# Turning x in a ring of four banks ahead of the edge counting, one-hots with the tile innermost, and window bounds loaded one window ahead

## The chip, the cores and the metric

The kernel runs on one core of a Trainium2 chip. The metric is the time of one execution on the device in microseconds. The text calls the engines by the names of the profile: PE is TensorE's matrix array and PEld its weight load, DVE is VectorE, ACT is ScalarE, POOL is GpSimd and SP is SyncE. Each engine has a sequencer that works through its instructions in order and hands the arithmetic to the engine behind it; register operations, branches and loads into registers are done by the sequencer itself.

## The reference

The graph has 1024 nodes and 16384 edges, sorted by destination. Two graph networks follow each other, each with a residual and a layer norm.

```python
edge_index = jnp.stack([src, dst])                     # 16384 edges, dst sorted
x = _layernorm(x + gat_two_layers(x, W1, a_src1, a_dst1, b1, W2, a_src2, a_dst2, b2, edge_index))
x = _layernorm(x + gcn_two_layers(x, W1, b1, W2, b2, edge_index))   # self loops, x 1024 x 768

def gat_layer(x, W, a_s, a_d, b, edge_index, concat):
    h = (x @ W).reshape(n, H, C)                       # first layer: 8 heads of 768
    alpha_s, alpha_d = einsum(h, a_s), einsum(h, a_d)
    e = leaky_relu(alpha_s[src] + alpha_d[dst], 0.2)
    e = exp(e - segment_max(e, dst)[dst])
    alpha = e / (segment_sum(e, dst)[dst] + 1e-16)
    return segment_sum(h[src] * alpha, dst) + b

def gcn_conv(x, W, b, src, dst, n_nodes):
    h = x @ W
    norm = dinv[src] * dinv[dst]                       # dinv = 1 / sqrt(degree)
    return segment_sum(h[src] * norm, dst) + b
```

The kernel never gathers by edge. It first builds a dense table countT of how many edges go from each source to each destination, and every later sum over edges is a matmul with that table.

## The kernel before

The change lies in the first stage, `graph_and_heads`, which does two things before its large matmuls: it counts the edges, and it turns x.

**Counting.** The edges lie in 128 tiles of 128, one edge per partition. From each edge two keys are made. The low key is the source modulo 128. The other key holds the block of the source and the destination; it is compared against 512 lanes for each of 16 windows of 64 destinations (`WD`, `NW`). A one-hot of the low key is the stationary operand and a one-hot of the other key the moving one of a 128x128 by 128x512 matmul, and the sum over the edge tiles that can touch the window is the window's part of countT. All low one-hots are made before the first window: `hot_low` is a table of 128 columns for each tile, in groups of 8 tiles (`TG`). ACT makes the first `ACT_TILES` tiles, a group in two steps: 8 times |lane - key| into `far` (L473), then one Relu of 1 - far over 128x1024 (L478). DVE makes the rest with one comparison over 128x1024 for each group (L737). The other one-hots, `hot_key`, are made by DVE window by window, in two buffers, 8 firm tiles (L749) and then pairs of tiles in a loop (L754) whose end is read from a register; in most windows this loop runs once.

**PE's part of a window** (from L1066): two loads of registers from `range_i`, the first tile and the end of the loop (L1067, L1068, each `value_load` is a load, a register operation and an assertion); 8 matmuls (L1076); a loop of pairs of matmuls (L1080, L1083); and a small matmul with zeros that closes the sum (L1085). ACT then copies the window's bank to countT (L511). DVE's part has the same two loads in front (L744, L745).

**Turning x.** x is needed with its features on the partitions, in two parts, xTh (rounded) and xTl (what is left). There are 12 groups g of 128x512 (6 blocks of features, 2 halves of the nodes). For each, PE turns four blocks of x into bank g modulo 4 (`turn_x`, L1047), ACT copies the bank to xTh (`x_high`, L487), PE subtracts xTh from the bank (`lessen_x`, L1055), and ACT copies what is left to xTl (`x_low`, L491). `turn_x(g)` for g of 4 and more waits until `x_low(g - 4)` has emptied the bank. Three groups are turned before the first window (`X_BEFORE`); then window w turns group w + 3 and lessens group w, after its closing matmul.

**Order.** Each engine runs its instructions in the order written. PE, before the counting, waits for ACT's last column copy (L506, behind all of ACT's low one-hots), turns three groups, then waits for both engines' low one-hots. The tables of lanes are written by POOL's iota instructions at the very start (L440 to L442), followed by the identity (L443, L445), which PE needs for every transpose and so for the keys. After the last window PE waits for countT and starts the large matmuls of q = 0 (L1106), in which 12 column blocks by 8 row blocks follow each other. The remaining stages (attention, second layer, graph convolution) are bound to that start by their data.

## Time and profile before

| | us |
|---|---|
| median of three timed runs | 1778.51 |
| lowest and highest of them | 1774.86, 1779.06 |
| the profiled execution, whole time | 1777.28 |
| its span, first to last instruction | 1775.2 |
| PE busy in the span | 1673.4 (94%) |
| first matmul of x's turning | 19.37 |
| closing matmul of the first window | 25.97 |
| closing matmul of the last window | 79.11 |
| first large matmul (L1106) | 80.09 |

The span is counted from the first instruction, and all times of the trace are offsets from it. The chain of waits in the page is almost wholly PE's, so a microsecond in front of 80.09 is a microsecond of the whole. A stretch of the trace is best read in the order of time, engine by engine; the sequencer's own instructions stand under PEldq and DVEq in the view of one source line.

### The profile page before, as it was taken

The page shows a single profiled execution, that of the slowest core. Times are in us where ns is not written, and L with a number is a line of the kernel's source. Part 1 is how long each engine was busy: PE and PEld are TensorE (multiplying, and loading weights), DVE is VectorE, ACT ScalarE, POOL GpSimd, SP SyncE. Part 2 cuts the span into 40 slices and gives each one's busy share as a digit, 9 for nine tenths or more (in the row PEclk, how much of TensorE's full clock was granted, in tenths as well). Part 3 has the DMA queues.
Part 4 walks back from the last instruction along what each step waited for, and adds up shares of the span by engine and source line. Part 5 has one row for each costly group of instructions (what it writes and reads, how often), then busy time and mean ns, then how long its engine had stood idle before and what let it go on. Part 6 is the DMA issues. An engine that isn't in the chain of part 4 may idle for free. (4 is left out here: it accounts for less than half of the span.)

```text
span 1775.2 us, 21747 instructions
## 1 busy us (share of the span) xinstructions
PE 1673.4 (94%) x7596; PEld 1393.4 (78%) x7601; DVE 1223.8 (69%) x2336; ACT 798.1 (45%) x1295; POOL 164.7 (9%) x117
## 2 busy tenths in 40 slices
PE   5899999999979999999999899999999975879998
PEld 3588888788857888888888688888888864878898
DVE  8744454654787887788877687888767348974447
ACT  6333321222545565565555455655556225534240
POOL 0023221312200000000000000000000013210003
PEclk9999999999989999999999999999999977989999
DMA  3155575766535765557654765666344321131222
GB/s 135 42 184 184 180 235 167 172 226 205 199 114 197 191 185 148 149 176 213 173 125 173 198 158 160 178 187 168 122 171 182 112 110 36 54 127 55 63 83 105
DMA packets 133808, 268.04 MB, mean 151 GB/s; under 512 B 23738, under 2 KB 83524, under 8 KB 121028
## 3 DMA queue, kind: packets, MB, share of 16 engines
q1 hardware_dynamic: 133700, 266.63, 48.8%
q8 instruction: 63, 1.03, 0.2%
q14 instruction: 45, 0.37, 0.1%
HBM read 206.21 MB, written 60.40 MB: 150 GB/s over the span
## 5 line engine op out<-in xcount | busy, mean ns | idle before, releaser
L41 PE MATMUL bank<-ph,hc 128*128 128x512 f32 x768 | 300.2, 391 | 4.7 <-DMA hc<-h_scratch 3.5
L43 PE MATMUL bank<-ph,hc 128*128 128x512 f32 x768 | 299.5, 390 | 0.0
L42 PE MATMUL bank<-pl,hc 128*128 128x512 f32 x768 | 299.4, 390 | 0.0
L771 DVE CUSTOM_DVE_ANT_0 junk<-bank,a_bc 128x512 bf16<-128x512 f32 (+1 forms) x256 | 129.9, 554 | 195.3 <-ACT st L523 180.1
L41 PE MATMUL bank<-hh,w2h 128*128 128x512 f32 x576 | 226.2, 393 | 14.7 <-DVE w2l L853 10.3
L41 PE MATMUL bank<-wh,xTh 128*128 128x512 f32 x570 | 224.3, 393 | 4.7 <-POOL wl L458 4.7
L43 PE MATMUL bank<-hh,w2l 128*128 128x512 f32 x576 | 225.7, 392 | 0.0
L42 PE MATMUL bank<-hl,w2h 128*128 128x512 f32 x576 | 225.5, 392 | 0.0
L43 PE MATMUL bank<-wh,xTl 128*128 128x512 f32 x570 | 223.3, 392 | 0.0
L42 PE MATMUL bank<-wl,xTh 128*128 128x512 f32 x570 | 223.1, 391 | 0.0
L41 PEld LDWEIGHTS bank<-ph,hc 128*128 128x128 f32 x768 | 144.5, 188 | 36.0 <-DMA hc<-h_scratch 3.9
L43 PEld LDWEIGHTS bank<-ph,hc 128*128 128x128 f32 x768 | 144.5, 188 | 30.1
L42 PEld LDWEIGHTS bank<-pl,hc 128*128 128x128 f32 x768 | 144.6, 188 | 30.0
L591 ACT ACTIVATE he<-mean,bias 128x512 f32<-128x512 f32 x96 | 69.6, 725 | 213.4 <-DVE mean L914 213.4
L523 ACT CAST st<-bank 128x512 fp32r<-128x512 f32 x96 | 56.5, 589 | 226.3 <-PE bank L43 218.2
L41 PEld LDWEIGHTS bank<-hh,w2h 128*128 128x128 f32 x576 | 109.2, 190 | 38.4 <-issue 10.7
L41 PEld LDWEIGHTS bank<-wh,xTh 128*128 128x128 f32 x570 | 107.9, 189 | 28.0 <-POOL wl L458 5.6
L42 PEld LDWEIGHTS bank<-hl,w2h 128*128 128x128 f32 x576 | 109.1, 189 | 22.9
L43 PEld LDWEIGHTS bank<-hh,w2l 128*128 128x128 f32 x576 | 109.0, 189 | 23.0
L43 PEld LDWEIGHTS bank<-wh,xTl 128*128 128x128 f32 x570 | 107.7, 189 | 22.6
L42 PEld LDWEIGHTS bank<-wl,xTh 128*128 128x128 f32 x570 | 107.8, 189 | 22.2
L914 DVE TENSOR_TENSOR mean<-bank,rden 128x512 f32<-128x512 f32 x96 | 66.0, 687 | 83.4 <-PE bank L43 83.4
(257 smaller groups left out, 2867.6 us busy)
## 6 DMA issues: line engine op xcount, KB each, us to landing
hc<-h_scratch SPq DMA_DIRECT2D x96, 1024.0 KB, 5.4
h_scratch<-st SPq DMA_DIRECT2D x96, 512.0 KB, 3.0
w2r<-in_L_gnn_W SPq DMA_DIRECT2D x96, 384.0 KB, 6.6
wr<-in_L_gnn_W SPq DMA_DIRECT2D x12, 1536.0 KB, 8.7
gwr<-in_L_gnn_W SPq DMA_DIRECT2D x24, 384.0 KB, 3.2
row_bc<-logits_scratch SPq DMA_DIRECT2D x16, 512.0 KB, 13.1
expo_bc<-expo_scratch SPq DMA_DIRECT2D x16, 512.0 KB, 6.2
xr<-in_x SPq DMA_DIRECT2D x2, 1536.0 KB, 8.4
```

What stands on the lines that cost most here:

```text
L41: nc.tensor.matmul(out, sh, mh, start=first, stop=False, skip_group_check=not grouped)
L42: nc.tensor.matmul(out, sh, ml, start=False, stop=False, skip_group_check=not grouped)
L43: return nc.tensor.matmul(out, sl, mh, start=False, stop=last, skip_group_check=not grouped)
L523: nc.scalar.copy(st[n % 4][:, :, 0, :], banks[n % 6][:, :].rearrange("p (g c) -> p g c", g=4)).then_inc(main_hi, 1)
L591: nc.scalar.activation(he[:, g % 2, :], mean[:, g % 2, :], ACT.Exp, bias=b)
L771: nc.vector.tensor_tensor_reduce(out=junk[:, s % 2, 0:hi - lo], in0=banks[n % 6][:, lo:hi], in1=a_bc[q % 2][:, k, lo:hi], scale=1.0, scala ...
L914: nc.vector.tensor_tensor(mean[:, g % 2, :], banks[6 + g % 2][:, :], rden[:, :], ALU.mult).then_inc(a_out, 1)
```

## The change

The diff does six things.

- **ACT makes 24 tiles of low one-hots rather than 32**, and DVE 104 rather than 96.
- **hot_low has the tile innermost.** The element of tile t and column l lies at l * 128 + t rather than t * 128 + l. ACT's Relu reads `far` with a step of 128 elements and writes runs of 8; DVE's comparison writes runs of 8, and reads a written-out table `lanes` (128 lanes, each 8 times, 16 bits) and `key16`, the low key in 16 bits, 8 elements again and again. PE's weight load takes 128 columns with a step of 128 elements.
- **The lane table** costs an iota of 128x1024 on POOL, in front of the identity's last step, and a cast to 16 bits on DVE, in front of upto_end. `key16` costs ACT one more copy of the key's bank.
- **x is turned in a ring of four.** Before the first window PE turns groups 0 to 3, lessens 0 to 3 and turns 4 to 7, behind the keys but no longer behind ACT's column copies. Then window w lessens group w + 4 (w below 8) and, after that, turns group w + 8 (w below 4).
- **The bounds of a window** are loaded one window ahead on PE and DVE, between the 8 firm tiles and the loop.
- ACT's order follows: x_high 0 to 3, x_low 0 to 3, x_high 4 to 7, and in window w, behind the copy to countT, x_low(w + 4) and x_high(w + 8).

```diff
-ACT_TILES = 32
+ACT_TILES = 24
-    hot_low = put("hot_low", 86016, [P, 2 * ET, P], BF16)
+    hot_low = put("hot_low", 86016, [P, 2 * ET * P], BF16)
+    lane_t = put("lane_t", early + 13312, [P, P, TG], I32)
+    lanes = put("lanes", early + 17408, [P, P, TG], F16)
+    key16 = put("key16", early + 19456, [P, P], F16)
-    X_BEFORE = 3
+    XA = 4
+    def low_tiles(j):
+        return hot_low[:, 0:P * ET].rearrange("p (l t) -> p l t", t=ET)[:, :, j * TG:(j + 1) * TG]
...
             nc.gpsimd.memset(ident[:, :], 0.0).then_inc(const_g, 1)
+            nc.gpsimd.iota(lane_t[:, :, :], pattern=[[1, P], [0, TG]], base=0, channel_multiplier=0).then_inc(lanes_made, 1)
             pool.wait_ge(const_g, 4)
...
             def low_hot_end(j):
                 act.wait_ge(far_done, j + 1)
-                nc.scalar.activation(hot_low[:, j * TG:(j + 1) * TG, :].rearrange("p t l -> p (t l)"), far[:, j % 2, :, :].rearrange("p t l -> p (t l)"),
+                nc.scalar.activation(low_tiles(j), far[:, j % 2, :, :].rearrange("p t l -> p l t"),
                                      ACT.Relu, bias=ones[:, 0:1], scale=-1.0).then_inc(low_hot_s, 1)
...
             nc.scalar.copy(keyT[:, 1, 0:P], banks[5][:, 0:P]).then_inc(key_out, 1)
+            nc.scalar.copy(key16[:, :], banks[5][:, 0:P]).then_inc(key16_out, 1)
...
-            for g in range(X_BEFORE):
+            for g in range(XA):
+                x_high(g)
+            act.wait_ge(range_done, 9)
+            for g in range(XA):
+                x_low(g)
+            for g in range(XA, 2 * XA):
                 x_high(g)
             for w in range(NW):
                 act.wait_ge(count_full, w + 1)
                 nc.scalar.copy(countT[:, :, w * WD:(w + 1) * WD], count_bank(w)[:, :].rearrange("p (s d) -> p s d", s=NB)).then_inc(count_out, 1)
-                if w < XG:
-                    if w + X_BEFORE < XG:
-                        x_high(w + X_BEFORE)
-                    x_low(w)
+                if w + XA < XG:
+                    x_low(w + XA)
+                if w + 2 * XA < XG:
+                    x_high(w + 2 * XA)
...
+            dve.wait_ge(lanes_made, 1)
+            nc.vector.tensor_copy(lanes[:, :, :], lane_t[:, :, :]).then_inc(lanes_made, 1)
             dve.wait_ge(const_v, 3)
             nc.vector.tensor_scalar(upto_end[:, :], upto[:, :], -1.0, float(EP), ALU.mult, ALU.add).then_inc(const_v, 1)
...
             for j in range(ACT_TILES // TG, ET // TG):
-                nc.vector.tensor_tensor(hot_low[:, j * TG:(j + 1) * TG, :],
-                                        lane[:, 0:P].unsqueeze(1).to_broadcast([P, TG, P]),
-                                        keyT[:, 1, j * TG:(j + 1) * TG].unsqueeze(2).to_broadcast([P, TG, P]), ALU.is_equal).then_inc(low_hot_v, 1)
+                nc.vector.tensor_tensor(low_tiles(j), lanes[:, :, :], key16[:, j * TG:(j + 1) * TG].unsqueeze(1).to_broadcast([P, P, TG]),
+                                        ALU.is_equal).then_inc(low_hot_v, 1)
...
-            pe.wait_ge(range_done, 9)
-            pe.wait_ge(cols_done, 3)
             pe.wait_ge(low_out, 1)
             pe.wait_ge(const_c, 4)
-            for g in range(X_BEFORE):
+            for g in range(XA):
                 turn_x(g)
+            for g in range(XA):
+                lessen_x(g)
+            for g in range(XA, 2 * XA):
+                turn_x(g)
+            pe.wait_ge(range_done, 9)
+            following = bounds(0)
+            pe.wait_ge(cols_done, 3)
             pe.wait_ge(low_hot_s, ACT_TILES // TG)
             pe.wait_ge(low_hot_v, (ET - ACT_TILES) // TG)
             for w in range(NW):
-                first = pe.value_load(range_i[w:w + 1, 0:1], min_val=0, max_val=ET - SLOTS)
-                pairs = pe.value_load(range_i[w:w + 1, 1:2], min_val=FIRM // 2 + 1, max_val=EP)
+                first, pairs = following
...
-                    mm = nc.tensor.matmul(bank[:, :], hot_low[:, bass.ds(first + j, 1), :].rearrange("p t l -> p (t l)"), hot_key[w % 2][:, j, :],
+                    mm = nc.tensor.matmul(bank[:, :], hot_low[:, bass.ds(first + j, P, ET)], hot_key[w % 2][:, j, :],
                                           start=(j == 0), stop=False, skip_group_check=True)
...
+                if w + 1 < NW:
+                    following = bounds(w + 1)
                 with pe.Fori(FIRM // 2, pairs) as q:
...
-                if w < XG:
-                    if w + X_BEFORE < XG:
-                        turn_x(w + X_BEFORE)
-                    lessen_x(w)
+                if w + XA < XG:
+                    lessen_x(w + XA)
+                if w + 2 * XA < XG:
+                    turn_x(w + 2 * XA)
```

DVE's window loop is changed as PE's is: its two loads go behind the eight firm tiles.

## Rows read from the trace of the kernel before

**Rows 1.** PE in order of time, windows that turn x: start, length, instruction, tiles.
```profile
36.20 0.22 PE L1085 MATMUL bank<-zero_b 128*128 128x128 bf16 x1
...
37.12 0.48 PE L1055 MATMUL bank<-xTh,neg_ident 128*128 128x512 f32 x1
...
39.77 0.22 PE L1085 MATMUL bank<-zero_b 128*128 128x128 bf16 x1
```
**Rows 2.** PE in order of time, the last window and the close before it, without x.
```profile
75.76 0.22 PE L1085 MATMUL bank<-zero_b 128*128 128x128 bf16 x1
76.94 1.90 PE L1076 MATMUL bank<-hot_key,hot_low 128*128 128x512 bf16 x8 [0.96 <-ACT countT L511]
...
79.11 0.22 PE L1085 MATMUL bank<-zero_b 128*128 128x128 bf16 x1
```
**Rows 3.** PE's source lines, one window: durations min/median/max in ns, first and last start.
```profile
L1067 PEldq TENSOR_LOAD <-range_i x1: 306/306/306, 72.1 to 72.1; - x1
...
L1076 PEldq FUSED_REGOPS  x8: 55/55/60, 73.5 to 74.4; - x8
L1076 PEld LDWEIGHTS bank<-hot_key,hot_low x8: 95/97/97, 73.6 to 74.9; 128*128 x8
...
L1080 PEldq COMPARE_BRANCH  x1: 70/70/70, 75.2 to 75.2; - x1
```
**Rows 4.** PE in order of time, the long window's closing matmul and one two windows later.
```profile
44.29 0.22 PE L1085 MATMUL bank<-zero_b 128*128 128x128 bf16 x1
...
52.00 0.22 PE L1085 MATMUL bank<-zero_b 128*128 128x128 bf16 x1
```
**Rows 5.** ACT in order of time, behind the closing matmul at 36.20.
```profile
36.45 0.59 ACT L511 CAST countT<-bank 128x512 int16<-128x512 f32 x1 [0.87 <-PE bank L1085]
37.40 0.59 ACT L487 CAST xTh<-bank 128x512 fp32r<-128x512 f32 x1 [0.36 <-PE bank L1047]
37.88 0.59 ACT L491 CAST xTl<-bank 128x512 fp32r<-128x512 f32 x1
```
**Rows 6.** POOL and then DVE in order of time, the tables and the first key.
```profile
0.83 0.55 POOL L440 IOTA lane_i<- 128x512 int32 x1 [0.39 <-POOLq L1887]
1.35 0.44 POOL L441 IOTA pair_i<- 16x128 int32 x1
...
1.95 0.43 DVE L685 CAST lane<-lane_i 128x512 f16<-128x512 int32 x1
...
3.39 0.23 DVE L695 TENSOR_SCALAR parts_i<-edge_i 128x128 int32<-128x128 int32 x1
```
**Rows 7.** ACT in order of time, its low one-hots and its last column copy.
```profile
5.17 4.78 ACT L473 ACTIVATE far<-lane,keyT 128x128 f16<-128x128 f16 x16
...
16.90 2.17 ACT L478 ACTIVATE hot_low<-far,ones 128x1024 bf16<-128x1024 f16 x2
...
19.11 0.16 ACT L506 COPY gcn_bias<-bank 128x6 f32<-128x6 f32 x1
```
**Rows 8.** PE in order of time, x's first three groups and the first window's close.
```profile
19.37 4.54 PE L1047 MATMUL bank<-ident,xr 128*128 128x128 f32 x24 [12.56 <-ACT gcn_bias L506]
...
25.97 0.22 PE L1085 MATMUL bank<-zero_b 128*128 128x128 bf16 x1
```
**Rows 9.** DVE in order of time, its low one-hots and eight firm tiles of a window.
```profile
8.02 13.69 DVE L737 TENSOR_TENSOR hot_low<-lane,keyT 128x1024 bf16<-128x1024 f16 x12
...
34.99 2.19 DVE L749 TENSOR_SCALAR hot_key<-lane,keyT 128x512 bf16<-128x512 f16 x8 [0.31 <-issue]
```
**Rows 10.** The tile xr, its two loads: last line is DMA from issue to landing, min/median/max.
```profile
L352 SPq DMA_DIRECT2D xr<-in_x x2: 401/454/507, 3.2 to 3.6; - x2
...
DMA to landing us min/median/max: 6.7/8.4/10.2
```
**Rows 11.** Windows of PE at a pause: stretch and length, busy (instructions), granted clock, DMA.
```profile
316.00:318.76 2.76, 0.61 (x4) 1.00 0.88 294
318.76:323.20 4.44, 4.44 (x12) 0.62 0.00 0
```

More of the change, by code:

```diff
@@ L236, in graph_and_heads @@
     hot_free = [sem(f"hot_free{w}") for w in range(NW)]
-    x_less = sem("x_less")
+    x_less, lanes_made, key16_out = sem("x_less"), sem("lanes_made"), sem("key16_out")
     count_full, count_out = sem("count_full"), sem("count_out")
@@ L733, in _, with bounds @@
             nc.vector.tensor_copy(range_i[:, :], range_f[:, 2:4]).then_inc(range_done, 1)
[L735 removed]
+            dve.wait_ge(key16_out, 1)
+            dve.wait_ge(lanes_made, 2)
             for j in range(ACT_TILES // TG, ET // TG):
[L737 to L739 removed]
+                nc.vector.tensor_tensor(low_tiles(j), lanes[:, :, :], key16[:, j * TG:(j + 1) * TG].unsqueeze(1).to_broadcast([P, P, TG]),
+                                        ALU.is_equal).then_inc(low_hot_v, 1)
             dve.wait_ge(range_done, 9)
             dve.wait_ge(low_out, 1)
+            def bounds(w):
+                return (dve.value_load(range_i[w:w + 1, 0:1], min_val=0, max_val=ET - SLOTS),
+                        dve.value_load(range_i[w:w + 1, 1:2], min_val=FIRM // 2 + 1, max_val=EP))
+            following = bounds(0)
             for w in range(NW):
[L744 to L745 removed]
+                first, pairs = following
                 if w >= 2:
@@ L1056, in lessen_x, with bounds @@
                                  start=False, stop=True, skip_group_check=True).then_inc(x_less, 1)
-            pe.wait_ge(range_done, 9)
-            pe.wait_ge(cols_done, 3)
+            def bounds(w):
+                return (pe.value_load(range_i[w:w + 1, 0:1], min_val=0, max_val=ET - SLOTS),
+                        pe.value_load(range_i[w:w + 1, 1:2], min_val=FIRM // 2 + 1, max_val=EP))
             pe.wait_ge(low_out, 1)
             pe.wait_ge(const_c, 4)
-            for g in range(X_BEFORE):
+            for g in range(XA):
                 turn_x(g)
+            for g in range(XA):
[3 more added lines that the diff above has]
+            pe.wait_ge(range_done, 9)
+            following = bounds(0)
+            pe.wait_ge(cols_done, 3)
             pe.wait_ge(low_hot_s, ACT_TILES // TG)
@@ L1066, in _ @@
             for w in range(NW):
-                first = pe.value_load(range_i[w:w + 1, 0:1], min_val=0, max_val=ET - SLOTS)
-                pairs = pe.value_load(range_i[w:w + 1, 1:2], min_val=FIRM // 2 + 1, max_val=EP)
+                first, pairs = following
                 bank = count_bank(w)
@@ L1079, in _ @@
                         mm.then_inc(hot_free[w + 1], SLOTS)
+                if w + 1 < NW:
+                    following = bounds(w + 1)
                 with pe.Fori(FIRM // 2, pairs) as q:
@@ L1082, in _ @@
                         pe.wait_ge(hot_ready[w], q * 2 + (j + 1))
-                        nc.tensor.matmul(bank[:, :], hot_low[:, bass.ds(q * 2 + first + j, 1), :].rearrange("p t l -> p (t l)"), hot_key[w % 2][:, FIRM + j, :],
+                        nc.tensor.matmul(bank[:, :], hot_low[:, bass.ds(q * 2 + first + j, P, ET)], hot_key[w % 2][:, FIRM + j, :],
                                          start=False, stop=False, skip_group_check=True).then_inc(hot_free[w], 1)
                 nc.tensor.matmul(bank[:, 0:P], zero_b[:, 0:P], zero_b[:, 0:P], start=False, stop=True, skip_group_check=True).then_inc(count_full, 1)
-                if w < XG:
-                    if w + X_BEFORE < XG:
-                        turn_x(w + X_BEFORE)
-                    lessen_x(w)
+                if w + XA < XG:
+                    lessen_x(w + XA)
+                if w + 2 * XA < XG:
+                    turn_x(w + 2 * XA)
             pe.wait_ge(x_lo, XG)
```

3 lines of the change are left out of this document (removed).

## The prediction

> **What bounds the kernel now.** I read the page first: its chain of waits is PE from end to end. The part that the change touches ends with the last window's closing matmul at 79.11 [rows 2]; one copy later PE starts its large matmuls, and what follows is fed from there, so I count a shift of that row one for one. The timeline from 0 to 85 us shows two stretches: a preparation that ends with the first window's closing matmul at 25.97 [rows 8], and the counting.
>
> Within the counting, the first windows, which turn x, close 3.45 us apart (four from 25.97 to 39.77) [rows 1, 8], and windows without x 3.35 apart (75.76 to 79.11) [rows 2]. Nearly the same, though the first kind has over 1 us more of matmul work. The view of PE's source lines explains it. In one window without x the first register load starts at 72.1, the eight firm matmuls get their addresses from 73.5 to 74.4, and the loop's branch comes at 75.2 [rows 3]. The sequencer is at work throughout: some 1.3 us for the two bounds, 1.1 for the eight firm tiles, 0.8 for the loop and the close, with rounding 3.35. It waits for nobody. Outside the x windows the bound is thus PE's sequencer, not its array, and the reader should see that the array's idle time in front of L1076 is the price of instructions, not of a wait.
>
> DVE makes its eight firm tiles in 2.19 us [rows 9] and with pair and loads stays below PE's period; it is not the bound.
>
> **Part 1: bounds loaded one window ahead.** This moves two loads in a sequencer that never waits in such a window. Its work stays 3.35, so the period stays 3.35. Three things are gained. The last window carries no loads any more: between its predecessor's close and its own lie ten matmuls and a start (from 76.94 to 79.11 are 2.17) [rows 2], 2.4 us, so -0.95. The one window with a second pass of the loop is followed today by two disturbed ones: from 39.77 to 52.00 [rows 1, 4] are 12.23 us, where three regular windows take 10.35. The second pass itself, 44.29 less 39.77 less 3.45 [rows 1, 4], is 1.1 us and stays; the other 0.8 is the loads of PE and DVE standing in line behind it, and goes. Windows 8 to 11, which carry parts of x today and will not, save up to 0.1 each, 0.3 together. The gain is 0.95 + 0.8 + 0.3, some 2.0 us. As bounds: none of it (0), or, were the loads hidden altogether in the seven windows up to the last but one, 0.3 more in each, since DVE's own period (2.19, and some 0.8 around it) is then next: 4.1.
>
> **Part 2: the ring of four banks.** Here I expect the loss. Today window w turns group w + 3, whose bank was emptied one window earlier. After the change window w lessens group w + 4 and then turns group w + 8 into the same bank. The turn must wait until ACT has emptied it, and ACT starts that copy, x_low(w + 4), only behind the copy of this very window to countT, which waits for the closing matmul. The new wait stands on PE, and all of the next window is queued behind it, address work and matmuls. Its length from the closing matmul: 0.25 until ACT starts (36.20 to 36.45) [rows 1, 5], 0.48 from one ACT copy to the next (37.40 to 37.88) and 0.59 for x_low [rows 5], and 0.10 from the end of an ACT copy to PE's next start (19.11 and 0.16 to 19.37) [rows 7, 8]: 1.42. Only then can the sequencer go on with the window's 3.24 us of loads, tiles, loop and close. The period is 4.7. The array alone would need 1.42, 0.87 for the turn (36.20 to 37.12 are 0.92, with some 0.05 of the closing matmul) [rows 1] and 2.17 for ten matmuls [rows 2], 4.5, so the sequencer still decides. Four periods at 4.7 stand where 13.8 us stood: +5.0. If the array's figure decides, +4.2; if the wait were hidden wholly, 0. I take 5.0, since each term is a row.
>
> **Part 3: the tables.** The new iota stands in front of the identity on POOL, and its cast on DVE in front of the keys. An iota of 512 elements in one run takes 0.55 us, 1.1 ns an element; pair_i, 128 elements in runs of two, takes 0.44, 3.4 ns an element [rows 6]. The new one has 1024 elements in 128 runs of 8. Bounds: 1.1 and 3.5 us. With 1.0 ns an element and some 4.5 a run, which fits both rows, it is 1.6; I take that, as its runs lie between the two. It starts near 1.9 and ends at 3.5. The cast then holds DVE for 0.60 (twice the elements of L685, whose 0.43 has about 0.15 of start) [rows 6], three small instructions take 0.5, and L695 starts at 4.7 rather than 3.39 [rows 6]: the keys are 1.3 late (0.8 to 3.2). Both chains of one-hots hang on them. The copy to key16 is short and lies in ACT's wait for its own first copy; I count 0, at most 0.2.
>
> **Part 4: ACT's chain to the first window.** ACT drops a group of 8 far (0.30 each, 4.78 for 16) and a Relu (1.04, half of the 2.17 for two) [rows 7]: -3.4. With the keys 1.3 late its last column copy ends near 17.1, not 19.27. Today PE waits for that copy and turns x from 19.37 [rows 8]. After the change PE turns groups 0 to 3 when x's first half lands, at 3.2 + 6.7 = 9.9 [rows 10], under ACT's one-hots. But x_high(0) still stands behind these, at 17.2. Four x_high at 0.48 bring x_low(0) to 19.1 and its end to 19.7, and turn 4 starts at 19.85. Four turns at 0.87 are 3.5 us. The first window could start at 23.4, and its close, held by the sequencer's first loads behind x_low(3), come at 25.85: -0.1 against 25.97 [rows 8]. The 2 us that ACT gained are used up by the ring's first round.
>
> The clock adds to that. PE's first turns ran at the lower rate: 24 in 4.54 us [rows 8], where eight later ones, one group, take 0.87 [rows 1]. After a stretch in which PE was busy for 0.61 of 2.76 us, the mean granted clock of the next 4.44 us was 0.62 [rows 11], mostly the 1.2 of the two levels, 1.2 and 2.4 GHz. The new kernel has turned its four groups by about 15.2 and pauses until the first lessening at 17.9, 2.7 us. I expect the same fall; over the turns of groups 4 to 7 it costs about 1.2 us. The first window starts at 24.6 and its ten matmuls close at 26.8: +0.85. That is my value; -0.1 is the other end.
>
> **Part 5: the new layout.** DVE's comparisons are 12 in 13.69 us, 1.14 apart, and 16-bit work at another line makes 512 elements in 0.27 (2.19 for eight) [rows 9], so 1024 cost at least 0.5. Thirteen take 6.9 to 14.8 us from 9.3 on and end between 16 and 24.1. I take 0.6 each and an end at 17, as all operands become runs of 16-bit elements like those of that row. Either way ACT's chain, 24.6, is later: DVE's gain is off the path, and the slow end costs up to 0.7. For ACT's Relu with a step of 128 elements there is no row: between no change and twice its time per element I take no change. PE's weight load takes 97 ns [rows 3] under a matmul of 217 (2.17 us for ten) [rows 2]; with its new step I take it as hidden.
>
> On this layout the Trainium skill, "Advanced Engine Details and Errata", section SBUF Cachelines, speaks against the change: full rate needs another access in the same 16-byte line, and a new line for each access is slower. By it the Relu's reads and PE's weight columns, one element a line, would pay; no run here shows such a step yet. On DVE's comparison the skill's "Vector Engine (DVE) Microarchitecture Reference", section 5.1, says that two-source work on 2-byte elements at step 1 yields two a cycle; at its 0.96 GHz that is, as an estimate, 0.53 us and a start.
>
> **The sum.** Preparation +0.85, ring +5.0, windows -2.0: +3.9 us. Against the profiled execution's 1777.28 this is 1781.2. The median of the runs, 1778.51, lies 1.2 above that execution, and the forecast for a median is 1782.4.
>
> **The rivals.** *The forecast*, a net 1 to 5.3 us, 0.59.
> *Strided reads cost ACT (slower).* A Relu's time per element is 1.04 less 0.30 over the 896 elements that it has beyond a far [rows 7], 0.83 ns. If each costs twice, three Relus are 0.85 longer, +2.6 us, all on the chain to x_high(0): 1785.0. It decides the verdict from 0.5 us a Relu on. For it: each read is 256 bytes from the last; against it: no row shows a cost. 0.22.
> *The weight load becomes the bound (slower).* Up to 217 ns it hides, and up to 0.33 the sequencer's 3.35 covers it. At 0.45 each window's ten need 4.5: +1.2 in twelve windows, 1796. 0.05.
> *The ring's wait is hidden (no change).* Part 2 is then 0: 1777.4, and 1776.5 without the fall of the clock. For it: PE's sequencer runs ahead of its array. Against it: the wait starts at the closing matmul itself. 0.09.
> *The loads are hidden too (faster).* With Part 1 at -4.1, the ring hidden and the preparation at -0.1 it is 1774.3. 0.05.
>
> 0.3%, about what a measurement of this kernel can tell from no change, is 5.3 us. The forecast lies inside, with about a sixth beyond the edge; the slower rivals go mostly beyond: slower 0.32, faster 0.05, within 0.63. The range for 8 in 10 takes in the iota's upper bound or the Relus above and a hidden ring below: 1776.5 to 1788.
>
> **What would show it.** Closing matmuls 4.7 apart in the first four windows, with turns (L1047) that wait for ACT's copy to xTl; 3.35 apart in the last eight although the loads stand elsewhere; 2.4 before the last; L695 near 4.7; comparisons 0.6 apart; the first closing matmul at 26.8, and a granted clock below 1.00 between 19 and 22. The prediction is wrong if the first periods are near 3.5, if the last fall towards 3.0 (then the sequencer was not the bound), or if Relus or weight loads grow.

## The result, and the profile after

The changed kernel takes 1787.51 us (median; 1784.28 to 1789.29) where the kernel before takes 1778.51. The ratio is 1.0049, interval 1.0037 to 1.0061: 9 us slower. The forecast was 3.9 us slower. The direction is the forecast's, and 1787.5 is inside the range of 1776.5 to 1788, though by half a microsecond only. The loss is 2.3 times the forecast's, and beyond the 0.3% within which the prediction had put its 0.63.

The profiled execution of the changed kernel has a span of 1785.9 us, and the first large matmul starts at 88.41 instead of 80.09. These 8.3 us account for nearly all of the 9.0 between the medians. These are the marks of the two traces beside those of the prediction (us from the span's start; the predicted fifth and last are added up from its first closing matmul, its period of 4.7 and its gain of 2.0):

| mark | before | predicted | after |
|---|---|---|---|
| first key instruction | 3.39 | 4.7 | 5.08 |
| first closing matmul | 25.97 | 26.8 | 30.99 |
| fifth closing matmul | 39.77 | 45.6 | 49.78 |
| last closing matmul | 79.11 | 82.9 | 87.42 |

From first to fifth the change costs 4.99 us (forecast 5.0), from fifth to last it gains 1.70 (forecast 2.0). The preparation costs 5.02 where the forecast had 0.85. That is where the prediction missed.

**The tables.** POOL and DVE in order of time; [rows 6] answer to it. Columns in all timelines: start, length, engine, line, instruction.
```profile
1.31 2.16 DVE L694 CAST ones_r<-ones 128x128 fp32r<-128x128 f32 x1
...
1.92 1.82 DVE L698 CAST lane<-lane_i 128x512 f16<-128x512 int32 x1
1.99 1.40 POOL L450 IOTA lane_t<- 128x1024 int32 x1
...
3.96 0.68 DVE L702 CAST lanes<-lane_t 128x1024 f16<-128x1024 int32 x1
...
5.08 0.21 DVE L710 TENSOR_SCALAR parts_i<-edge_i 128x128 int32<-128x128 int32 x1
```
The iota takes 1.40 us (estimate 1.6). Two DVE casts that were begun when it started both end just behind its end: the cast of lane takes 1.82 us instead of 0.43 [rows 6].

**ACT, DVE and PE up to the first window.** In order of time; [rows 7 to 9] answer to it.
```profile
6.84 4.78 ACT L480 ACTIVATE far<-lane,keyT 128x128 f16<-128x128 f16 x16
...
9.68 7.92 DVE L753 TENSOR_TENSOR hot_low<-lanes,key 128x1024 bf16<-128x1024 f16 x13
10.02 5.30 PE L1068 MATMUL bank<-ident,xr 128*128 128x128 f32 x32 [1.54 <-DMA xr<-in_x]
...
11.53 2.09 ACT L485 ACTIVATE hot_low<-far,ones 128x1024 bf16<-128x1024 f16 x1
...
16.00 3.98 ACT L485 ACTIVATE hot_low<-far,ones 128x1024 bf16<-128x1024 f16 x2
...
20.71 2.25 PE L1076 MATMUL bank<-xTh,neg_ident 128*128 128x512 f32 x4 [5.39 <-ACT xTh L494]
...
22.75 5.70 PE L1068 MATMUL bank<-ident,xr 128*128 128x128 f32 x32
...
30.99 0.22 PE L1116 MATMUL bank<-zero_b 128*128 128x128 bf16 x1
```
A far costs what it did, 0.30 us. A Relu, the instruction at L485, takes about 2.05 us where [rows 7] have two in 2.17. DVE's thirteen comparisons take 7.92 us, 0.6 each, and end at 17.6; PE's first window, which needs them, starts at 28.29. PE pauses for 5.39 us in front of its first lessening, and its turns of groups 4 to 7 then take 5.70.

The granted clock tells why. Stretches of PE: length, busy (instructions), granted clock, DMA.
```profile
15.00:19.70 4.70, 0.32 (x3) 1.00 1.04 350
19.70:22.70 3.00, 1.99 (x4) 0.54 0.20 74
22.70:26.50 3.80, 3.80 (x19) 0.50 0.00 0
```
0.50 is the 1.2 GHz level. Stretches cut at finer times show it from 19.97, 0.7 us before PE's restart, to 26.80, and 1.00 behind that.

**The ring.** PE and then ACT around the second closing matmul; [rows 1, 5] answer to it.
```profile
35.73 0.22 PE L1116 MATMUL bank<-zero_b 128*128 128x128 bf16 x1
35.76 0.48 PE L1076 MATMUL bank<-xTh,neg_ident 128*128 128x512 f32 x1
37.11 1.16 PE L1068 MATMUL bank<-ident,xr 128*128 128x128 f32 x8 [0.87 <-ACT xTl L498]
```
```profile
35.98 0.59 ACT L524 CAST countT<-bank 128x512 int16<-128x512 f32 x1 [1.44 <-PE bank L1116]
36.47 0.59 ACT L498 CAST xTl<-bank 128x512 fp32r<-128x512 f32 x1
```
The turn starts 1.38 us behind the closing matmul (working: 1.42) and waits for ACT's copy to xTl. The first four periods are 4.74, 4.66, 4.64 and 4.75.

**The windows without x.** PE's firm matmuls in one such window by source line (ns min/median/max), then the last window in order of time; [rows 3] and [rows 2] answer.
```profile
L1105 PEld LDWEIGHTS bank<-hot_key,hot_low x12: 208/208/211, 75.9 to 79.8; 128*128 x12
L1105 PEldq FUSED_REGOPS  x10: 46/46/53, 76.0 to 79.4; - x10
```
```profile
85.00 0.22 PE L1116 MATMUL bank<-zero_b 128*128 128x128 bf16 x1
85.14 2.02 PE L1105 MATMUL bank<-hot_key,hot_low 128*128 128x512 bf16 x7
...
87.42 0.22 PE L1116 MATMUL bank<-zero_b 128*128 128x128 bf16 x1
```
The weight load has doubled, from 97 to 208 ns, and stays just below the matmul's 217. The address instruction has become cheaper, 46 ns for 55. The period is 3.26 to 3.28 instead of 3.35, the last one 2.42.

### The profile page after: what moved, and what is told of

It reads as the page before. It is cut to its first block and busy times, and to the rows that moved or that the text cites. A ratio compares the mean times of both kernels' runs of the same rounds, so it can differ in the third digit from the quotient of the medians.

```text
span 1785.9 us, 21744 instructions
## 1 busy us (share of the span) xinstructions
PE 1684.1 (94%) x7596; PEld 1413.5 (79%) x7601; DVE 1225.9 (69%) x2338; ACT 802.4 (45%) x1287; POOL 167.2 (9%) x118
## 5 line engine op out<-in xcount | busy, mean ns | idle before, releaser
L42 PEld LDWEIGHTS bank<-pl,hc 128*128 128x128 f32 x768 | 144.6, 188 | 29.9
```

Of the source, the lines that this page charges most:

```text
L42: nc.tensor.matmul(out, sh, ml, start=False, stop=False, skip_group_check=not grouped)
```

## The experiments

Each kernel was timed in three rounds against the kernel before on the same chip. The ratio is to the kernel before, with its 95% interval; the closing matmuls and the first large matmul are from the profiled execution.

| kernel | ratio | first | fifth | last close | large matmuls |
|---|---|---|---|---|---|
| before | 1 | 25.97 | 39.77 | 79.11 | 80.09 |
| changed | 1.0049 [1.0037, 1.0061] | 30.99 | 49.78 | 87.42 | 88.41 |
| ring_late | 1.0016 [1.0006, 1.0025] | 30.61 | 44.53 | 82.41 | 83.40 |
| relu_dense | 1.0058 [1.0042, 1.0075] | 34.60 | 53.30 | 90.88 | 91.87 |
| tables_late | 1.0036 [1.0023, 1.0048] | 30.27 | 48.86 | 86.51 | 87.49 |
| kept_warm | 1.0025 [1.0014, 1.0036] | 29.59 | 48.30 | 85.69 | 86.68 |
| loads_ahead | 0.9993 [0.9983, 1.0002] | 26.21 | 39.85 | 78.05 | 79.04 |
| loads_held | 1.0035 [1.0023, 1.0046] | 33.34 | 52.12 | 87.12 | 88.10 |
| recast | 0.9965 [0.9950, 0.9980] | 22.34 | 36.25 | 74.13 | 75.11 |
| recast_held | 0.9975 [0.9966, 0.9985] | 25.67 | 39.52 | 75.06 | 76.05 |
| layout_old | 1.0041 [1.0029, 1.0052] | 27.27 | 47.46 | 85.59 | 86.57 |
| recast_old | 0.9996 [0.9986, 1.0007] | 27.48 | 41.26 | 79.36 | 80.34 |
| recast_two | 0.9977 [0.9966, 0.9989] | 25.01 | 38.87 | 75.53 | 76.51 |

The last column less 80.09 and the difference in time that the ratio gives agree within about 2 us in every row (recast: -5.0 and -6.2; ring_late: +3.3 and +2.9; relu_dense: +11.8 and +10.3; kept_warm: +6.6 and +4.5). To within these 2 us a shift of the first large matmul is handed on to the time. The times alone do not part loads_ahead and recast_old from the kernel before, nor tables_late, loads_held, layout_old and relu_dense from the changed one; for these the closing matmuls speak. Spans of single profiled executions scatter more behind that point, and I rest nothing on them.

### The ring: the turn one window later

```diff
-                if w + XA < XG:
-                    lessen_x(w + XA)
-                if w + 2 * XA < XG:
-                    turn_x(w + 2 * XA)
+                if 1 <= w and w - 1 + 2 * XA < XG:
+                    turn_x(w - 1 + 2 * XA)
+                if w + XA < XG:
+                    lessen_x(w + XA)
```
(and ScalarE's x_high and x_low in the same order)

> The changed kernel with its turning moved one window later: window w turns group w + 7 (w from 1 to 4), whose bank was emptied in the window before, and then lessens group w + 4. Theory of the ring: PE no longer waits for ACT's copy to xTl behind its own closing matmul, so from the first to the fifth closing matmul it takes about 13.9 us rather than 18.8, the first large matmul comes 5 us earlier than in the changed kernel (near 83.4), and the time falls by about 5 us. Rival, the slower weight load (209 ns) fills the array in windows that turn x: the periods fall only to 3.7 or more, 14.8 in all. Rival, the periods are the address work's and the loads': nothing changes.

ring_late is 5.0 us less than the changed kernel at the first large matmul. The fence has PE and ACT in order of time around a window's start.
```profile
33.87 0.22 PE L1116 MATMUL bank<-zero_b 128*128 128x128 bf16 x1
33.93 1.11 PE L1068 MATMUL bank<-ident,xr 128*128 128x128 f32 x8
...
34.13 0.59 ACT L524 CAST countT<-bank 128x512 int16<-128x512 f32 x1 [1.45 <-PE bank L1116]
```
The turn now starts 0.06 us behind the close, into a bank that ACT emptied a window ago. Four periods are 13.92 us instead of 18.79. The ring's wait is the cause of these 4.9 us; the first closing matmul came 0.38 sooner besides.

### The Relu: reads in one run

```diff
-    far = put("far", early + 3072, [P, 2, TG, P], F16)
+    far = put("far", early + 3072, [P, 2, P, TG], F16)
...
-                    last = nc.scalar.activation(far[:, j % 2, i, :], lane[:, 0:P], ACT.Abs, bias=keyT[:, 1, tile:tile + 1], scale=-1.0)
+                    last = nc.scalar.activation(far[:, j % 2, :, i], lane[:, 0:P], ACT.Abs, bias=keyT[:, 1, tile:tile + 1], scale=-1.0)
...
-                nc.scalar.activation(low_tiles(j), far[:, j % 2, :, :].rearrange("p t l -> p l t"),
+                nc.scalar.activation(low_tiles(j), far[:, j % 2, :, :],
```

> The changed kernel with far laid out with the tile innermost, so that the Relu reads without a step and |lane - key| is written with a step of 8 elements (16 bytes); hot_low is written as before. Theory, the read at 256 bytes a step is what made the Relu 2.05 us: the three Relus are back at 1.13, far stays 0.30 each, ACT's chain is 2.8 us shorter and the first large matmul near 85.6. Rival, the runs of 8 that are written cost: Relus stay at 2.05, nothing moves. Rival, the cost goes over to the writes of far: Relus 1.13 but far 0.4 or more each, over 2.4 us back.

ACT in order of time:
```profile
6.84 9.45 ACT L480 ACTIVATE far<-lane,keyT 128x128 f16<-128x128 f16 x16
15.78 1.36 ACT L485 ACTIVATE hot_low<-far,ones 128x1024 bf16<-128x1024 f16 x1
...
21.52 2.37 ACT L485 ACTIVATE hot_low<-far,ones 128x1024 bf16<-128x1024 f16 x2
```
With reads in one run a Relu is 1.36, 1.34 and 1.13 us, so the 256-byte read step was its cost. The two longer ones start while the last far is still under way (the first at 15.78, where the fars end at 16.29). The third stands behind a Relu and takes the 1.13 of the kernel before, though it writes in runs of 8 like the others. But far, which now writes each element 16 bytes behind the last, goes from 0.294 to 0.54 us apiece. Twenty-four of these lose 5.9 us where the Relus gained 2.3, and the kernel is slower still: its first closing matmul comes at 34.60. This is the rival that had the cost go over to far. Of the two places tried the transposition costs less in the Relu, once for eight tiles.

### The table: POOL's iota behind the identity

```diff
+            nc.gpsimd.iota(lane_t[:, :, :], pattern=[[1, P], [0, TG]], base=0, channel_multiplier=0).then_inc(lanes_made, 1)
```
(moved from ahead of the identity's last step to behind it; its cast moved from ahead of the keys to ahead of the comparisons; ACT waits for it in front of x_low(0))

> The changed kernel with the lane table's iota behind the identity's last step on POOL and its cast to 16 bits on DVE just in front of the comparisons, behind the keys. Theory: the first key instruction is back near 3.4 (5.08 in the changed kernel), the cast of ones is back at 0.56 us (2.16), and the first window, which hangs on ACT's chain, starts 1.7 us earlier; the comparisons end where they did and stay off the path. The first large matmul is near 86.7. Rival: DVE's comparisons now decide and nothing is gained; rival: POOL's iota slows DVE's key instructions beside it, and part of the 1.7 stays.

POOL and DVE in order of time:
```profile
1.31 0.56 DVE L695 CAST ones_r<-ones 128x128 fp32r<-128x128 f32 x1
...
1.95 0.43 DVE L699 CAST lane<-lane_i 128x512 f16<-128x512 int32 x1
...
2.49 1.41 POOL L453 IOTA lane_t<- 128x1024 int32 x1
2.52 1.40 DVE L701 CAST win_f<-win_i 128x16 f32<-128x16 int32 x1
...
4.49 0.21 DVE L709 TENSOR_SCALAR parts_i<-edge_i 128x128 int32<-128x128 int32 x1
```
The casts of ones and lane are back at 0.56 and 0.43. Now the cast that happens to lie beside the iota stands: sixteen elements take 1.40 us, where the changed kernel needs 0.15 for them. So DVE does not merely queue behind the iota's result; a cast that has nothing to do with it waits until POOL is done. The keys came at 4.49, not at 3.4: 0.59 us sooner than in the changed kernel. The first large matmul gained 0.92 of the expected 1.7; PE's pause was shorter besides, 4.00 us, and its turns of groups 4 to 7 took 5.26 us instead of 5.70. On this the Trainium skill, "Advanced Engine Details and Errata", section Mode Summary, has a note: VectorE's second SBUF port is shared with GpSimd, and GpSimd's instructions and VectorE's two-port ones block each other. The trace agrees, with 0.15 against 1.40 us. The prediction had not weighed it.

### The clock: PE kept busy in its pause

```diff
+            pe.wait_ge(range_done, 2)
+            for _ in range(22):
+                nc.tensor.matmul(banks[7][:, :], zero_b[:, 0:P], zero_b[:, :], start=True, stop=True, skip_group_check=True)
             for g in range(XA):
                 lessen_x(g)
```

> The changed kernel with 22 matmuls of zeros (128x512, 16 bits, a bank whose content has been read) in PE's pause between the turning of group 3 and the lessening of group 0. Theory of the clock: the granted clock stays at 1.00 there, the 32 matmuls that turn groups 4 to 7 take about 3.6 us rather than 5.7, and the first large matmul comes 2 us earlier, near 86.3. Rival: these turns are paced by ACT's copies, the clock has no part, and nothing moves.

The same stretches as above, and PE's turns of groups 4 to 7:
```profile
19.70:22.70 3.00, 3.00 (x13) 1.00 0.20 78
22.70:26.50 3.80, 3.80 (x35) 1.00 0.01 2
```
```profile
22.73 3.84 PE L1068 MATMUL bank<-ident,xr 128*128 128x128 f32 x32
```
The clock stays at 1.00 and the turns take 3.84 us instead of 5.70. The first lessening is 0.4 us later, since the zero matmuls run on beyond the pause. The first window starts 1.9 us sooner and closes 1.40 sooner, and the first large matmul is 1.73 us sooner. The low clock costs the changed kernel 1.9 us in its turns.

### The loads alone, on the kernel before

```diff
-                first = pe.value_load(range_i[w:w + 1, 0:1], min_val=0, max_val=ET - SLOTS)
-                pairs = pe.value_load(range_i[w:w + 1, 1:2], min_val=FIRM // 2 + 1, max_val=EP)
+                first, pairs = following
...
+                if w + 1 < NW:
+                    following = bounds(w + 1)
                 with pe.Fori(FIRM // 2, pairs) as q:
```
(and the same on VectorE)

> The kernel before with one part of the change alone: PE and DVE load a window's two bounds one window ahead. Theory (PE's sequencer is the bound, and a load costs it the same wherever it stands): periods of windows without x stay 3.35 us, the last is 2.4 instead of 3.35, the two windows behind the one with a second pass lose their 0.8 us; the last closing matmul comes at 77.3 instead of 79.11, the first large matmul at 78.3 instead of 80.09, and the time falls by 1.8 us. Rival 1 (the loads become hidden, because the array or DVE was the bound): periods without x fall to about 3.0, some 4 us less in all. Rival 2 (the place of the loads is worth nothing): all closings as before, 0.

The end of PE's timeline:
```profile
75.64 0.23 PE L1097 MATMUL bank<-zero_b 128*128 128x128 bf16 x1
...
78.05 0.22 PE L1097 MATMUL bank<-zero_b 128*128 128x128 bf16 x1
```
Of first to last closing matmul 1.30 us are gone, not 1.75. The last period is 2.41, the two before it are 3.36 and 3.34: a load costs PE's sequencer the same at either place. But the three periods over the long window still take 12.04 us, where [rows 1, 4] have 12.23. Of the 0.8 that I expected there, 0.2 came. In the time the kernel can't be told from the one before.

No run isolates why those two windows stay long, but the trace of the changed kernel points at DVE (in order of time):
```profile
53.29 0.69 DVE L775 TENSOR_SCALAR hot_key<-lane,keyT 128x512 bf16<-128x512 f16 x2 [4.53 <-PE bank L1114]
53.83 2.39 DVE L768 TENSOR_SCALAR hot_key<-lane,keyT 128x512 bf16<-128x512 f16 x8
```
The second pass of the loop writes into the pair of buffers that the first pass filled, so DVE stands for 4.53 us until PE has used them. Its lead is gone, it makes the next window's eight tiles only now, and PE, which closed the long window at 54.47, takes them at DVE's pace. That the loads stood in line there was not the main cost.

### Is the sequencer the bound? Bounds held in registers

```diff
+            pe.wait_ge(range_done, 9)
+            held_bounds = {v: bounds(v) for v in range(NW - 8, NW)}
             for g in range(XA):
                 lessen_x(g)
...
-                    following = bounds(w + 1)
+                    following = held_bounds[w + 1] if w + 1 in held_bounds else bounds(w + 1)
```
(loads_held: on PE; on VectorE behind its comparisons)

> The changed kernel, but the bounds of the last eight windows are loaded earlier and held in registers: PE's while it pauses after its first turns, DVE's behind its comparisons. Theory (PE's sequencer sets the period of windows without x, the array and the doubled weight load are covered): the periods into the last eight windows fall from 3.26 to about 2.7, DVE's own period or the array's 2.4 being next; the last closing matmul comes some 4 us sooner against the first one, and the time falls by about 4 us if the first window is not later. Rival (the weight load at 0.21 us with a matmul pace of 0.235 us, or DVE, is already the bound): the periods stay at or above 3.2, and nothing is gained.

Periods fall from 3.26 to 2.66, 2.66, 2.86 and then 2.9 to 3.1, so the sequencer was the bound. But eight windows' loads take PE longer than its pause: the first closing matmul comes 2.35 us later, and in time the two can't be told apart (1.0035 against 1.0049, with intervals that overlap). Where the clean figure is seen is recast_held, the same idea on recast (below) for the last six windows, PE and then DVE in order of time:

> As recast, with the bounds of the last six windows loaded early and held, on PE around its first turns and on VectorE beside and behind its comparisons. Theory (the sequencer is the bound of windows without x): against recast the last six periods are 2.7 instead of 3.27, 3 us less, if the first window is not later by the loads' own time (VectorE's six loads of two bounds, about 0.65 us a window, 2 us of them behind the comparisons). So between 1 and 3 us below recast. Rival (the array with the strided weight load is the bound): the periods stay at 3.2 and the kernel is 0 to 2 us slower than recast.

```profile
60.64 0.22 PE L1121 MATMUL bank<-zero_b 128*128 128x128 bf16 x1
60.70 1.99 PE L1110 MATMUL bank<-hot_key,hot_low 128*128 128x512 bf16 x8
...
62.95 0.22 PE L1121 MATMUL bank<-zero_b 128*128 128x128 bf16 x1
```
```profile
62.12 2.57 DVE L771 TENSOR_SCALAR hot_key<-lane,keyT 128x512 bf16<-128x512 f16 x8
...
65.12 2.57 DVE L771 TENSOR_SCALAR hot_key<-lane,keyT 128x512 bf16<-128x512 f16 x8
```
With no loads a window takes 2.31 us, with the weight load at 209 ns: the array's own rate. Two such windows use up DVE's lead, and from there DVE's period holds PE at 3.1. That is 3.0 us from one window's first tile to the next one's, not the 2.7 I expected: eight tiles take 2.57 here instead of the 2.19 of [rows 9], for a reason that no run shows. So the windows' three limits are 2.3 (array), 3.0 (DVE) and 3.26 (sequencer), and taking the sequencer away is worth 0.2 us a window once DVE's lead is gone. The loads cost recast_held 3.3 us at its first close, and its clock fell on the way; it is no better than recast.

### A kernel from the findings

```diff
-ACT_TILES = 24
+ACT_TILES = 16
-            nc.gpsimd.iota(lane_t[:, :, :], pattern=[[1, P], [0, TG]], base=0, channel_multiplier=0).then_inc(lanes_made, 1)
-            nc.vector.tensor_copy(lanes[:, :, :], lane_t[:, :, :]).then_inc(lanes_made, 1)
+            nc.vector.tensor_copy(lanes[:, :, :], lane[:, 0:P].unsqueeze(2).to_broadcast([P, P, TG])).then_inc(lanes_made, 2)
...
-            for g in range(XA, 2 * XA):
-                turn_x(g)
...
-                if w + XA < XG:
-                    lessen_x(w + XA)
-                if w + 2 * XA < XG:
-                    turn_x(w + 2 * XA)
+                if w + XA < XG:
+                    turn_x(w + XA)
+                if 1 <= w and w + XA - 1 < XG:
+                    lessen_x(w + XA - 1)
```
(and ScalarE's x_high and x_low in the same order)

> A kernel built from what the runs so far showed. No lane table from POOL: VectorE copies it from lane, repeated eight times, just before its comparisons. ScalarE has 16 tiles of one-hots instead of 24, VectorE 14 comparisons. Four groups of x are turned and lessened ahead; window w then turns group w + 4 into the bank that the window before has emptied, and lessens group w + 3. Theory (late keys, long Relus, the ring's wait and the clock together are the loss, and each goes with its own cause): the key instruction starts at 3.4 us as in the kernel before, comparisons run from about 8.6 to 17 us, the first closing matmul comes at 20 to 21 us, x windows are 3.55 apart and the others 3.27, the last closing matmul is at about 71 us instead of 79.1, and the time is some 8 us below that of the kernel before. Rival 1 (the repeated copy, reading one element eight times over, or the cold clock in the first windows costs it): first close at 22 to 24, gain 4 to 6 us. Rival 2 (a later stage takes the gain back, as the x groups' loads or weights arrive no sooner): the closings as in the theory, but a gain below 3 us in the time.

recast is faster than both: 0.9965 [0.9950, 0.9980] of the kernel before. That is 6 us by the ratio; the two medians, 1779.32 and 1783.54, lie 4.2 apart. I had expected 8. PE in order of time, and its stretches from the end of the lessenings:
```profile
18.30 0.22 PE L1096 MATMUL bank<-zero_b 128*128 128x128 bf16 x1 [1.26 <-DVE hot_low L749]
...
21.76 0.74 PE L1108 MATMUL bank<-hot_key,hot_low 128*128 128x512 bf16 x2 [1.14 <-issue]
...
22.34 0.22 PE L1110 MATMUL bank<-zero_b 128*128 128x128 bf16 x1
```
```profile
17.04:18.30 1.26, 0.00 (x1) 1.00 1.01 351
18.30:22.34 4.04, 2.85 (x10) 1.00 0.41 150
```
The first window starts at 18.3, and no clock falls. The timeline names DVE's comparisons as what it waited for. They end at 17.64, though, and the view of PE's second load of the first window's bounds (L1077) has:
```profile
L1077 PEldq SEQ_ASSERT  x1: 18/18/18, 18.0 to 18.0; - x1
```
PE's sequencer was at these loads from 16.5 to 18.0, so here they end last, 0.4 us behind the comparisons. I had the close at 20 to 21; it is at 22.3. These loads are one part of it, keys that came 0.3 late in this execution another, and the third is that the second window's loads stand inside the first, which nothing hides there (1.14 us of issue). The close lies in the band of rival 1, but neither of its causes is there: the repeated copy took 0.67 us, and the clock stayed at 1.00. From there on the periods are as expected (3.55 with x, 3.25 to 3.28 in windows without).

> recast, with PE's bounds of the last two windows loaded between its lessenings and the first window, where it waits for VectorE's comparisons; VectorE's loads stay. Theory (PE's sequencer is the bound, and VectorE is ahead by up to two windows): the two periods before the last are 2.3 to 2.6 us instead of 3.26, the first window is 0 to 0.7 us later, and the last closing matmul comes 1 to 1.5 us sooner than recast's, at about 73. Rival (VectorE, whose own period with its loads is about 3.1 to 3.2, has no lead in the last windows): the periods stay at 3.1 or above, and the kernel is like recast or up to 0.7 us slower.

recast_two adds `held_bounds = {v: bounds(v) for v in (NW - 2, NW - 1)}` on PE ahead of the first window. Two periods at the end are 2.46 and 2.31, as expected, and the very last is 2.87, where DVE is the bound. But loading costs far more than the 0.7 us I allowed:
```profile
17.06:20.91 3.85, 0.01 (x1) 1.00 0.79 262
20.91:25.01 4.10, 4.10 (x12) 0.58 0.00 0
```
PE pauses for 3.85 us, in which its sequencer loads three windows' bounds, 1.3 us each, the price that the prediction read off [rows 3]. I had taken PE to be waiting for the comparisons there; it was not, as recast shows, so the two added windows' loads cost their full 2.6 us. Behind that pause the granted clock is 0.58. At the last close it is 1.4 us behind recast; in time the two can't be told apart.

### What the layout is worth

```diff
-                nc.vector.tensor_tensor(low_tiles(j), lanes[:, :, :], key16[:, j * TG:(j + 1) * TG].unsqueeze(1).to_broadcast([P, P, TG]),
-                                        ALU.is_equal).then_inc(low_hot_v, 1)
+                nc.vector.tensor_tensor(hot_low[:, j * TG:(j + 1) * TG, :],
+                                        lane[:, 0:P].unsqueeze(1).to_broadcast([P, TG, P]),
+                                        keyT[:, 1, j * TG:(j + 1) * TG].unsqueeze(2).to_broadcast([P, TG, P]), ALU.is_equal).then_inc(low_hot_v, 1)
```
(with hot_low, the Relu and PE's reads tile by tile again, and no table)

> The changed kernel with its layout undone: hot_low tile by tile again, VectorE's comparisons against keyT as before, no iota, no cast, no 16-bit keys; the order of x, the 24 tiles for ScalarE and the loads one window ahead stay. Theory (the layout costs this kernel more than it brings, because VectorE was off the path and ScalarE and the keys are on it): key instruction at 3.4 us, Relus 1.13 us, thirteen comparisons 1.135 us apart from 8.0 to 22.8, first closing matmul at 26 to 28 us instead of 30.99, ring 18.8 us for four as in the changed kernel, windows without x 3.35; last closing at about 84.5 instead of 87.4, the time 3 us below the changed kernel and 5 to 6 us above the kernel before. Rival (VectorE's slower comparisons, the last ending at 22.8, set the first window): first closing at 29 us or later, and the layout paid for itself.

The first closing matmul comes at 27.27, as expected, 3.7 us sooner, with Relus of 1.13 us. PE waits 0.93 us for DVE's last comparison; the turns of groups 4 to 7 take 3.84 us at full clock, as their pause is gone. But the fall of the clock is only put off, to the turn of the first window. Stretches of PE:
```profile
27.27:28.65 1.38, 0.51 (x3) 0.98 0.04 12
28.65:33.42 4.77, 4.77 (x19) 0.65 0.00 0
```
That window takes 6.15 us instead of 4.7. So 1.84 us are left at the first large matmul, of 3 expected: the layout, with its tables, costs the changed kernel some 2 us, with this exchange of one stall for another in it. In the time this is not seen: 1.0041 and 1.0049 have intervals that overlap. The last windows without x are 3.34 to 3.35 apart here, and the address instruction takes 55 ns again.

> recast with the layout undone in the same way, and 24 tiles for ScalarE instead of 16 (13 comparisons for VectorE). Theory (once nothing else stands in front of the first window, VectorE's comparisons do, and there the layout is worth its cost): comparisons end at 22.8 us instead of 17.6, the first closing matmul comes at about 27 us instead of 22.3, x windows are 3.41 apart instead of 3.55 (weight loads of 97 ns instead of 209), windows without x 3.35; the last closing at about 79 us instead of 74.1, and the time within 2 us of the kernel before. Rival (the gain of recast is all from the order of x and the loads, none from the layout): last closing at 74 to 76 us and a time like recast's.

In recast the sign turns. recast_old has the old layout and gives ACT 24 tiles of one-hots instead of 16, so DVE makes 13 comparisons instead of 14. PE waits for them until 22.91, and the last closing matmul comes at 79.36 instead of 74.13. As expected the kernel can't be told from the one before (0.9996), and it is 5.2 us behind recast. Some 4.6 of these are the later start; PE's pause of 4.75 us also leaves the clock at 0.50 from 22.90 to 27.50, which recast is spared. One thing goes the other way: windows with x are 3.41 apart, as in the kernel before, against 3.55 in recast. There the second matmul of a window starts 0.36 us behind the first (26.84, 27.19) instead of 0.23 (35.68, 35.90): the longer weight load is not hidden once a window. The same layout costs 2 us where DVE is off the path and brings 5 where DVE is on it.

## Why the prediction was half right

**What bounds the kernel: right.** Holding the bounds in registers took the period from 3.26 to 2.31, so PE's sequencer was the bound of windows without x. DVE's "2.19, and some 0.8 around it" has the size of the 3.0 that was then seen, in part by luck: the 3.0 holds no loads, and its eight tiles took 2.57. The working's three terms for the sequencer (1.3, 1.1, 0.8) add up to 3.2, short of the measured 3.35; nothing hangs on it.

**Part 1, loads: right in size by luck, two of three terms wrong.** The last window gave 0.93 (forecast 0.95). The 0.8 behind the long window came as 0.1 to 0.2, in the changed kernel and in loads_ahead alike; the trace points at DVE's lost lead. The 0.3 for windows 8 to 11 came as 0.1 at most: in layout_old, which has the new order of x and the old layout, the seven windows before the last take 23.66 us against 23.76. In the changed kernel they take 23.08. These 0.68 are in neither layout_old nor loads_ahead (23.75), so they come with the layout, whose address instruction takes 46 ns instead of 55. The prediction had no such term, and it stands where the other two failed: 1.7 us for 2.0.

**Part 2, the ring: right.** 4.99 us for 5.0, and ring_late gave them back. That the sequencer and not the array decides behind the wait holds only just: between the second and the third closing matmul the eight firm matmuls follow the turn without a gap, and only the last pair and the close wait for the sequencer, 0.1 us in all.

**Part 3, the tables: mis-sized.** The iota's 1.40 lies near its estimate, but the keys were 1.69 late, not 1.3. The working had DVE's earlier casts run beside the iota at no cost. They stood until it ended.

**Part 4, ACT's chain: the failed step, by a term of Part 5.** "Between no change and twice its time per element I take no change" was the wrong end. A Relu went from 1.13 to 2.05 us; three are 2.75 us more, all on the chain to x_high(0). That is the rival "Strided reads cost ACT", which had 2.6. It holds 2.75 of the 4.2 us by which the first closing matmul missed. The rule of the Trainium skill on 16-byte lines ("Advanced Engine Details and Errata", SBUF Cachelines) pointed there, with no size, and the traces agree at all three places: Relus 1.13 to 2.05 us, far's writes 0.294 to 0.54, weight loads 97 to 208 ns. I had given it 0.22 for want of a row.

**Part 4, the clock: right in kind, mis-sized.** Forecast was a pause of 2.7 us and 1.2 us of cost. The late Relus made the pause 5.39 and the turns 5.70 us against 3.84 at full clock: 1.9. With the late keys (0.4), the Relus (2.75), the clock (0.7) and the first window, which took 2.70 from its start to its close instead of 2.2, that makes 4.3, and 4.2 were missing. The first window's 0.5 is a cost of Part 1 that the working left out: PE's sequencer loads the second window's bounds inside the first, from 28.6 to 29.9, where it has no lead yet.

**Part 5, the comparisons: right.** 0.6 us each and an end at 17.6, off the path. Weight loads were hidden, as taken, in the changed kernel: its windows with x are 4.64 to 4.75 apart behind the second close, and so are layout_old's. Where no wait covers them, in recast's windows with x, they cost 0.14 us a window (3.55 against 3.41 in recast_old).

**The sum.** Ring and windows together missed by 0.3 us, the preparation by 4.2. That the measured 1787.5 still lies in the range owes more to its width than to the working: 0.63 stood on less than 0.3%, and 0.22 on the rival that came. That rival was itself too small, as a late ACT makes PE's pause longer and so the clock's cost larger: with the clock's 0.7 its 1785.0 would have been 1785.7.

## What to carry to other kernels

A layout that makes one engine's instruction dense makes others strided: list every reader and writer of the tile, and where no row shows a strided read, take the doubled time for each that lies on the path. A buffer ring shortened by doing work earlier puts the emptying copy on the path of whoever refills it; turning one window later cost nothing and gave 5 us. And an engine made faster is worth its cost only where it is last: the same layout lost 2 us in one order of work and won 5 in another. Last, where a timeline names an engine as what a start waited for, compare the end of its work with what the waiting engine's own sequencer was doing: in recast it was register loads.

## What the runs showed of the chip that I had not expected

- ScalarE: 1024 elements of 2 bytes read 256 bytes apart take 2.05 us instead of 1.13; 128 elements written 16 bytes apart take 0.54 instead of 0.294.
- TensorE: a weight load of 128 columns 256 bytes apart takes 208 ns instead of 97. Matmuls of 512 columns over it still start 0.217 us apart, except for the second of a window, which starts 0.36 us behind the first in recast's windows with x.
- VectorE: casts beside an iota on GpSimd last until it has ended: 16 elements 1.40 us instead of 0.15, 128 elements 2.16 instead of 0.56.
- The granted clock: PE idle for 1.26 us in recast, and it stayed at 1.00; idle for 3.85 us in recast_two, and its mean was 0.58 over the next 4.1 us; idle for 5.39 us in the changed kernel, and it was 0.50 from 0.7 us before the restart to 6.1 us behind it; in layout_old its mean was 0.65 over 4.8 us behind pauses of 0.93, 1.43 and 0.87 us around its first window, none longer.
